# Three layout turns taken off TensorE: VectorE 32x32 block transposes with a DRAM shuffle, and a new slot order

## The reference, cut to what matters

```python
k = x @ Wk.T; v = x @ Wv.T                  # 16 heads of 32
k = k * cos + rotate_half(k) * sin
W = eye(32)                                  # per sequence and head
for each chunk of 16 tokens (256 in a row):
    z = kc @ W                               # this is the layer's output
    W = W - kc.T @ ((z - vc) * 2 / (16 * 32))
out = layernorm(z) * gamma + beta
x = layernorm(x + out @ Wo.T)
g = silu((x @ gate_w.T) * gate_s); u = (x @ up_w.T) * up_s
x = layernorm(x + ((g * u) @ down_w.T) * down_s)
```

## Time and profile before

| | us |
|---|---|
| median of 3 runs | 2064.01 (2063.62 to 2065.9) |
| the profiled execution, its own time | 2065.75 |
| its span in the trace | 2063.9 |
| TensorE (PE) busy | 1941.2, 94% |
| VectorE (DVE) busy | 1244.6, 60% |
| ScalarE (ACT) busy | 927.6, 45% |
| GpSimd (POOL) busy | 594.0, 29% |
| DMA, mean | 94 GB/s |

### The profile page before, as it was taken

The page is one execution under the profiler, slowest core; times in us unless marked ns, Lnnn a source line. Parts: engine busy times, 40 slices in busy tenths (PEclk is TensorE's granted clock), DMA queues, the critical chain, the costliest instruction groups (busy, mean ns, idle before and its releaser), DMA issues.

```text
span 2063.9 us, 54584 instructions
## 1 busy us (share of the span) xinstructions
PE 1941.2 (94%) x22424; PEld 1533.9 (74%) x22424; DVE 1244.6 (60%) x2814; ACT 927.6 (45%) x2258; POOL 594.0 (29%) x651
## 2 busy tenths in 40 slices
PE   3459999999999999999999999999999999999987
PEld 2237777777877777777777777777777787777775
DVE  2565666666566666656666665666666566666642
ACT  2225444444444444444444444444444444444432
POOL 1012323323332322333223233323323332332332
PEclk8669999999999999999999999999999999999998
DMA  9522332222233222223322222322222232222210
GB/s 327 182 84 63 104 100 76 94 85 80 87 105 98 78 89 90 77 90 104 97 78 86 94 75 92 104 90 84 88 88 81 91 104 90 81 90 73 85 41 21
DMA packets 236619, 193.38 MB, mean 94 GB/s; under 512 B 35217, under 2 KB 199313, under 8 KB 236177
## 3 DMA queue, kind: packets, MB, share of 16 engines
q1 hardware_dynamic: 233648, 172.56, 26.5%
q10 hardware_dynamic: 2720, 17.30, 2.3%
HBM read 105.86 MB, written 92.54 MB: 96 GB/s over the span
## 4 chain that ended last, share of the span: by engine, by line
PE 82%; DVE 7%; ACT 4%; issue 2%; DMA 2%; SPq 1%; POOL 0%; DVEq 0%; POOLq 0%; ACTq 0%
PE gu_acc L615 29%; PE work L596 26%; PE down_acc L627 15%; PE z_acc L569 4%; PE state_acc L584 4%; DVE err L795 3%; PE work L603 2%; ACT state L400 2%; PE gu_acc L603 2%; ACT hid L424 1%; DMA k_scr<-k_tok 1%; DVE fm L824 1%; DVE hid L802 1%; ACT fm L448 1%; SPq L230 1%
## 5 line engine op out<-in xcount | busy, mean ns | idle before, releaser
L795 DVE TENSOR_TENSOR err<-z_acc,v_rows 32x256 f32<-32x256 f32 x1024 | 429.6, 420 | 155.4 <-PE z_acc L569 105.7
L346 POOL TENSOR_TENSOR hid_lo<-hid,hid_hi 128x256 fp32r<-128x256 f32 x352 | 280.4, 797 | 777.3 <-ACT hid_hi L434 775.7
L400 ACT ACTIVATE state<-state_acc 32x256 f32<-32x256 f32 x1028 | 385.7, 375 | 197.5 <-PE state_acc L584 178.6
L615 PE MATMUL gu_acc<-x_hi,gw 128*128 128x256 f32 x1408 | 383.6, 305 | 6.8 <-DVE hid L802 3.3
L802 DVE SCALAR_TENSOR_TENSOR hid<-gu_acc,up_scale,hid 128x256 f32<-128x256 f32 x352 | 169.9, 483 | 297.8 <-ACT hid L424 293.9
L615 PE MATMUL gu_acc<-x_lo,gw 128*128 128x256 f32 x1408 | 347.6, 280 | 0.0
L615 PE MATMUL gu_acc<-x_lo,uw 128*128 128x256 f32 x1408 | 346.9, 279 | 0.0
L615 PE MATMUL gu_acc<-x_hi,uw 128*128 128x256 f32 x1408 | 346.9, 279 | 0.0
L615 PEld LDWEIGHTS gu_acc<-x_hi,gw 128*128 128x128 f32 x1408 | 264.8, 188 | 50.2 <-DVE hid L802 32.6
L627 PE MATMUL down_acc<-dw,hid_hi 128*128 128x512 f32 x704 | 289.8, 412 | 1.4 <-POOL hid_lo L346 1.4
L627 PE MATMUL down_acc<-dw,hid_lo 128*128 128x512 f32 x704 | 278.8, 396 | 0.0
(11 more groups left out here) (67 smaller groups left out, 2224.0 us busy)
## 6 DMA issues: line engine op xcount, KB each, us to landing
x_fm<-xT SPq DMA_DIRECT2D x64, 256.0 KB, 3.3
k_scr<-k_tok SPq DMA_DIRECT2D x32, 512.0 KB, 3.0
k_rows<-k_scr SPq DMA_DIRECT2D x512, 32.0 KB, 2.0
v_rows<-v_scr SPq DMA_DIRECT2D x512, 32.0 KB, 1.9
z_scr<-v_rows SPq DMA_DIRECT2D x32, 512.0 KB, 2.9
z_tok<-z_scr SPq DMA_DIRECT2D x512, 32.0 KB, 1.8
x_tok<-x SPq DMA_DIRECT2D x32, 512.0 KB, 3.9
out<-x_tok SPq DMA_DIRECT2D x32, 512.0 KB, 2.9
```

The lines of the kernel that those rows point to most:

```text
L346: pool.tensor_tensor(hid_lo[m % RING][:], hid[m % 2][:], hid_hi[m % RING][:].bitcast(F32), ALU.subtract).then_inc(hid_lo_ready, 1)
L400: act.activation(state[q, :, e].rearrange("p (r g) e -> p r g e", r=2), state_acc[q, :, 0:P].rearrange("p r (g e) -> p r g e", e=HEAD), AC ...
L615: mm = pe.matmul(gu_acc[:, k * TOK:(k + 1) * TOK], lhsT=w[:, c, m * P:(m + 1) * P].bitcast(dt), rhs=part[:, c].bitcast(dt), start=(c == 0 ...
L795: dve.tensor_tensor(err[q, g:g + 2, :, :].rearrange("p a (r h) e -> p a r (h e)", r=2), z_acc[q, :, 0:P].rearrange("p r (a c) -> p a r c", ...
```

## The change

- The 24 TensorE transposes of a tick are gone. VectorE turns 32x32 blocks (`turn`, one instruction for each b, six in a tick) from SBUF into one buffer, `turned`. SP stores it to DRAM in four transfers, one for each group of 32 partitions (`store_turned`), and loads it back in one, with the blocks in their places: `kT` for K, `landed` for z and for x1. A 128x128 turn is 16 block turns and this exchange of blocks.
- GpSimd copies `kT` to `k_cols` (now one buffer, in halves) in place of VectorE. `high_zn`, `low_zn`, `high_x1`, `low_x1` read SBUF (`landed`) in place of PSUM.
- New slots. Most of the feed-forward of block t-2 moves a tick later: in the tick that does its second norm only pieces 0 and 1 (slots 14, 15) remain. The b = 0 projections of block t move to the end of the tick ahead. The last norm of a block, `normalize(2, ...)`, moves from slot 14 to slot 0 of the next tick.
- The loops run from tick -1 to NT + 3, where they ran from 0 to NT + 2.
- SP issues 15 more transfers in a tick, and its order is new.

```diff
-FFN_SLOT = 10
-EARLY_GU, LATE_GU = {10: 0, 11: 1, 12: 2, 13: 3, 14: 4, 15: 5}, {0: 6, 1: 7, 2: 8, 3: 9, 6: 10}
+FFN_SLOT = 14
+EARLY_GU, LATE_GU = {14: 0, 15: 1}, {0: 2, 2: 3, 3: 4, 5: 5, 7: 6, 8: 7, 9: 8, 10: 9, 11: 10}
+EARLY_DOWN, LATE_DOWN = {15: 0}, {0: 1, 2: 2, 3: 3, 5: 4, 8: 5, 9: 6, 10: 7, 11: 8, 12: 9, 13: 10}
...
-            for t in range(NT + 3):
+            for t in range(-1, NT + 4):
                 tick(t)
...
+            def store_turned(scr, stored):
+
+                for a in range(HQ):
+                    sp.dma_start(scr[:, :, a].rearrange("h d g t -> d h (g t)"),
+                                 turned[a * HEAD:(a + 1) * HEAD].rearrange("d h g t -> d h (g t)")).then_inc(stored, 16)
...
+            def load_znT(n):
+                sp.wait_ge(znT_stored, 64 * (n + 1))
+                if n >= 1:
+                    sp.wait_ge(x1_lo_ready, 2 * n)
+                sp.dma_start(landed[:].rearrange("p a g t -> p (a g t)"),
+                             zT_scr.rearrange("h d a g t -> (h d) (a g t)")).then_inc(znT_in, 16)
...
+            def copy_k_cols(n, half):
...
+                a = slice(half * HQ // 2, (half + 1) * HQ // 2)
+                for p in range(2):
...
+                    pool.tensor_copy(dst, src).then_inc(k_cols_ready, 1)
...
+            def turn(src, b, done):
+
+                dve.transpose(turned[:, :, b * NC:(b + 1) * NC, :],
+                              src[:, b, :].rearrange("p (c h d) -> p h c d", c=NC, h=HQ)).then_inc(done, 1)
...
-                dve.tensor_tensor(x1_lo[:, :, b, :], gu_acc[:].rearrange("p (c t) -> p c t", c=NC),
-                                  x1_hi[:, :, b, :].bitcast(F32), ALU.subtract).then_inc(x1_lo_ready, 1)
+                dve.tensor_tensor(token_blocks(x1_lo, b), by_token(landed, b),
+                                  token_blocks(x1_hi, b).bitcast(F32), ALU.subtract).then_inc(x1_lo_ready, 1)
...
+                    if within(yn) and s == 0:
+                        normalize(2, yn, y_tok, y_tok, y_ready)
+                    if within(o) and s == 2:
+                        turn_zn(o, 0)
+                        turn_zn(o, 1)
...
+                    if within(t) and s == 6:
+                        turn_k(t, 0)
+                        turn_k(t, 1)
+                    if within(o) and s == 9:
...
+                        normalize(1, o, x1_tok[o % 2], x_tok, x1_ready)
+                        turn_x1(o, 0)
+                        turn_x1(o, 1)
```

More of the change, by code:

```diff
@@ L86, in build @@
         v_rows = sb("v_rows", [P, NS, 2, P])
-        k_cols = [sb(f"k_cols{i}", [P, NG, NS, 2 * MB]) for i in range(2)]
+        kT = sb("kT", [P, HQ, NG, HEAD])
+        k_cols = sb("k_cols", [P, HQ, NG, 2, 2 * MB])
         err = sb("err", [P, NG // 2, HQ, HEAD])
@@ L94, in build @@
         x1_tok = [sb(f"x1_tok{i}", [P, BATCH, DM]) for i in range(2)]
+        turned = sb("turned", [P, HQ, NG, HEAD])
+        landed = sb("landed", [P, HQ, NG, HEAD])
         x1_hi = sb("x1_hi", [P, NC, BATCH, P], F32R)
@@ L321, in tick @@
                 if within(sc):
-                    load_x(sc)
+                    load_v_half1(sc)
+                if within(o):
+                    load_x(o)
+                if within(t):
+                    store_v(t, 0)
+                if within(o):
+                    store_znT(o)
+                if within(t):
+                    store_k(t)
+                if within(o):
+                    load_znT(o)
+                if within(t):
+                    store_v(t, 1)
+                if within(sc):
+                    store_z(sc, 0, NS // 2)
+                if within(t):
+                    store_kT(t)
+                if within(sc):
+                    load_z(sc, 0, NS // 2, 16)
+                if within(t):
+                    load_kT(t)
+                    load_k_half0(t)
+                if within(o):
+                    store_x1T(o)
+                if within(t):
+                    load_v_half0(t, 0)
+                if within(o):
+                    load_x1T(o)
+                if within(t):
+                    load_v_half0(t, 1)
+                if within(t + 2):
+                    load_x_fm(t + 2)
+                if within(sc):
+                    store_z(sc, NS // 2, NS - 1)
+                    load_z(sc, NS // 2, NS - 1, 32)
+                    store_z(sc, NS - 1, NS)
+                    load_z(sc, NS - 1, NS, 48)
             run(tick)
@@ L599, in project @@
                     mm.then_inc(done, 1)
-            def turn(acc, src, b, done):
-                for c in range(NC):
-                    mm = pe.transpose(acc[:, c * P:(c + 1) * P], src[:, b, c * P:(c + 1) * P], eye[:])
-                mm.then_inc(done, 1)
             def gate_up(n, m, dt):
@@ L720, in tick @@
                         down(f1, EARLY_DOWN[s], ffn_dt)
-                    if t == 0 and s == 14:
-                        find_bias()
+                    if within(t + 1) and s in (13, 14):
+                        project_v(t + 1, 0, *((0, 3), (3, NC))[s - 13])
             def rest(ffn_dt):
                 tick(2, ffn_dt, FFN_SLOT, SLOTS)
-                for t in range(3, NT + 3):
+                for t in range(3, NT + 4):
                     tick(t, ffn_dt)
+            tick(-1)
             tick(0)
@@ L741, in _, with stats_of, moments_of @@
         def _(dve):
-            def moments_of(norm, n, src):
-                for b in range(BATCH):
-                    dve.bn_stats(stats[:, norm, b, :], src[:, b, :]).then_inc(stats_done[norm], 1)
+            def stats_of(norm, b, src):
+                dve.bn_stats(stats[:, norm, b, :], src[:, b, :]).then_inc(stats_done[norm], 1)
+            def moments_of(norm, n):
                 dve.wait_ge(stats_done[norm], 2 * n + 2)
@@ new lines, in tick @@
+                    if within(t + 1) and s == 11:
+                        low_x(t + 1, 1)
+                    if within(t + 1) and s == 13:
+                        rotate(t + 1, 0)
+                    if within(yd) and s == 13:
+                        scale_y(yd)
+                    if within(o) and s == 13:
+                        low_x1(o, 0)
+                        low_x1(o, 1)
+                    if within(yd) and s == 15:
+                        dve.wait_ge(y_added, 2 * yd + 2)
+                        stats_of(2, 0, y_tok)
+                        stats_of(2, 1, y_tok)
+                        moments_of(2, yd)
@@ L876, in tick @@
+                    if within(f2) and s in LATE_GU:
                         scale_hid(f2, LATE_GU[s])
-                    if within(f2) and s == 7:
-                        scale_hid(f2, 10)
                     if within(f1) and s in EARLY_GU:
@@ L916, in tick @@
                             low_part(wo, x1_tok, c, 2 * NC)
[L917 to L920 removed]
+                    for piece in WEIGHED.get((t, s), ()):
+                        weigh(piece)
+                    if t == 2 and s == 13:
                         dve.wait_ge(low_half_max, len(PIECES))
```

439 lines of the change are left out of this document (214 added, 225 removed).

## The result

Median of 4 runs 2123.12 us (2121.03 to 2128.82) against 2064.06 (2063.62 to 2065.9) for the kernel before: ratio 1.0289, 95% interval 1.0273 to 1.0306. The prediction said faster: 2018, with a range of 1981 to 2068. The direction, the size and the range were wrong.

A forecast was written before the change was run, and what follows sets the result against it. TensorE was taken to bound 28 or so of 35 ticks. Ticks 3 to 30 (-51.2), tick 31 (-3.6), start (-4) and tail (+12.8) took 2065.75 to 2019.75; the median, 1.7 lower, gave 2018, range 1981 to 2068.

The forecast's parts named there:

- The floor, 57.3: Middle tick: TensorE's 59.87 us of work less 2.6 for six transpose groups leaves 57.3 us.
- The block turn, 0.69: VectorE: each turn instruction takes 0.69 us, taken from another 128x512 float32 instruction; bounds 0.5 to 1.4.
- The rival of a slow turn: Slots 2, 7 and 9: turns of 1.4 us each lose 3.05 us a tick, giving 2106 us; chance 0.09.
- Slots 3 and 9, 0.45 and 0.37: Middle tick: TensorE waits for VectorE's `scale_hid`, 0.45 us ahead of slot 3's `gate_up` and 0.37 ahead of slot 9's.
- The z norm beside GpSimd's copy: Slots 0 to 3: VectorE's z norm meets GpSimd's K copies and ends at 7.4 us in place of 7.1.
- Slots 14 and 15, 0.1 + 0.2 + 0.1: Middle tick: TensorE stalls 0.1 us for slot 14's silu and `scale_hid`, 0.2 for slot 15's `copy_v`, 0.1 for `low_x1`.
- The rival that named it, 2047: x1's split meets GpSimd's residual add: `low_x1` pair ends 1.0 us later in 29 ticks, 2047 us; chance 0.19.
- z's detour, slack 1.4: Middle tick: turned z goes through DRAM and lands at 18.5 us, `high_zn` comes at 19.9; slack 1.4, cost nothing.
- The start, -4: First errors to tick 3's, 117.9 us before: 4 us shorter, ends -12 and +8.
- Tick 31 and the tail, -3.6 and +12.8: Tick 31 becomes 3.6 us shorter; the tail, where nothing hides the detours of z and x1, 12.8 longer.

The follow-up runs named there:

- e4_slots_only: Changed kernel with the second z turn, x1 turns and second norm's moments behind a `scale_hid`, half its statistics behind the scan's errors; 2104.32 us.
- e5_both: e1_late_residual plus the VectorE reordering of e4_slots_only; 2026.44 us.
- e2_memset: Changed kernel with GpSimd's residual add left out and a memset of a constant into the same tile in its place; 2045.29 us, one run.
- e1_late_residual: Changed kernel with GpSimd's residual add waiting until `low_x1` of the block behind it is done; 2044.89 us.
- e6_start: e5_both with the first weighing, VectorE's part of the reduction, the all-reduce and the FFN's loads some slots sooner; 2011.00 us.
- e10_z_before_k: e6_start with the load of the turned z issued on SP ahead of K's 512 KB store; 2009.35 us.
- e7_z_sooner: e5_both with VectorE's last norm behind the moments of z, and SP's loads of V and x moved around z's stores; 2064.44 us.
- e12_z_first: e10_z_before_k with VectorE's last norm behind z's moments, V's row loads ahead of out's store, x's load behind z's load; 2006.08 us.

## Why the prediction was wrong, point by point

- **The floor, 57.3.** Right: 57.29 to 57.39 of TensorE's work wherever the clock stayed at 1.00, and in the changed kernel 58.83 less the 1.5 that the slow `gate_up` took.
- **The block turn, 0.69.** Right: 0.682 to 0.691 in all three uses. The rival of a slow turn falls.
- **Slots 3 and 9, 0.45 and 0.37.** Right in place and nearly in size: 0.51 and 0.56. By e4_slots_only and e5_both both are worth 18 to 19 us together. The z norm beside GpSimd's copy was put 0.3 later; its pair took 1.13 against 1.00 for x's, so 0.13.
- **Slots 14 and 15, 0.1 + 0.2 + 0.1: the step that failed.** "`low_x1` ends when slot 14's `gate_up` wants it: 0.1" stands on a split at its free 0.69. It took 1.5, the wait was 1.96 in place of 0.1, and in 19 of 28 ticks the clock took 1.5 more, for which the sum had no term. Slot 15's 0.2 wasn't seen. The tick is then 57.3 + 0.51 + 0.56 + 1.96 + 1.5 = 61.8, measured 61.86; the mean of 61.58 has the ticks in which the clock held. With its clock this step makes most of the 91 us that the 29 ticks lie above the forecast.
- **The rival that named it, 2047.** The mechanism was there with its place, and got 0.19, priced at 1.0 a tick; measured 3.5 where the clock fell and 3.0 in the mean (1.96 and 1.04). Two errors made this. First the hold: GpSimd's pair was itself slowed (2.96 in place of 2.6), and the split ended 0.55 behind it, not 0.3. Second, and larger, the price ended with the wait. In the earlier trace rows there is already a `gate_up` of 3.16 behind an idle TensorE, and the windows of the start and the last tick have clocks of 0.78 and 0.90: a wait of 2 us should have been priced with the slow work behind it. With 3.0 in place of 1.0 the rival would have come to 2047 + 29 x 2.0 = 2105; the start and the tail, 7 and 11 above the forecast, are the other 18.
- **Its chance.** The norm beside two adds (2.92 against 0.99) was evidence that such a meeting costs a factor. The walk itself put both pieces into the same 2.6 us. Taking the two together, this should have been the forecast. The norm has one operand in SBUF beside its scalars, the split two, so the row showed such a hold but not that of the split. The Trainium skill (SBUF — State Buffer, Who interferes with whom) says it in a rule: two SBUF inputs on VectorE contend with a GpSimd instruction that reads SBUF. The trace agrees, 1540 ns against 688, and the write-only instruction of e2_memset leaves it at 688.
- **z's detour, slack 1.4.** The steps of the stores were too short. In the tick shown the four took 2.7 to issue (1.8 predicted) and had landed 4.8 after the first issue (3.6); the load took 3.5 (3.9). About 0.7 of slack was left there. In five other ticks of the changed kernel z was late, by 0.25 to 1.77 us and 4.0 in all, with the clock at 1.00 behind each; so "cost nothing" held nearly, and by a margin half as wide as forecast. With the other waits gone it is what remains (12 to 23 us of idle in e1_late_residual, e5_both, e6_start and e10_z_before_k).
- **The start, -4.** +3.0. The all-reduce beside TensorE's wait (6.2 us, where some 5 was forecast) was there as said; e6_start, which moves it with the weighing and the loads, gives 11.9 back. What made the other terms come out 6 us worse has no run of its own.
- **Tick 31 and the tail, -3.6 and +12.8.** The tail was +23.8. e1_late_residual has 151.0 for it, 6.4 less than 157.4: the split meets the add in the last two ticks too. The clock behind the waits for z and x1 (`project_o` 4.61 in place of 2.99, `gate_up` 3.42 in place of 2.16 in e5_both) is 2.9 of the other 4.6; the rest has no run of its own.

The forecast less the failed step is e1_late_residual: 58.65 in most ticks against 58.5. By the profiled spans it lies 25 us above the forecast: 7 of start, 5 of tail, and 13 in ticks, most of it in those with a late z.

## What to carry to other kernels

When an operand of a VectorE instruction moves from PSUM to SBUF, look up what GpSimd does in the same microseconds; if it reads SBUF there, delay it until VectorE is through, which cost nothing here and gave 78 us. Price a wait of TensorE of 2 us as the wait and the slow work that can follow it (1.5 us here, behind 19 of 28 such waits), and shorten or fill it before shorter ones are mended; a fill much longer than the wait costs what it gives. In an in-order DMA queue see what a moved instruction's consumer stands in front of: two VectorE instructions of half a microsecond, moved, became 120 us through SP.

## What the runs showed of the hardware

- VectorE with two SBUF operands beside a GpSimd add: 1540 to 1557 ns against 688, and GpSimd 1493 against 1291. Beside a GpSimd memset (526 ns): 688. A VectorE norm beside GpSimd copies: 1.13 against 1.00 for the pair. Block turns of x1 beside such copies: 1.29 for the pair, 1.30 alone. `scale_hid`, with one tile in PSUM and one in SBUF, beside the residual add of the kernel before: 0.48, as alone.
- The granted clock behind a wait of TensorE went with the wait's length, but not by it alone. Counted in the changed kernel and the twelve experiments, between 190 and 1840 us, with the clock of the 3.7 us behind each wait: 51 waits of 0.9 to 1.6 us, all at 1.00; 95 of 1.6 to 2.5 us, 29 at 1.00 and 66 lower; 25 of over 2.5 us, all lower. Single places: behind 1.38 us the clock was 1.00; behind 1.93, 1.96 and 2.85 us the next group took 4.38 (in place of 2.99), 3.59 (2.08) and 4.61 (2.99). So a late transfer can cost only its own wait in one tick and 1.4 us more in the next, as in the 58.7 and 62.0 of e1_late_residual.
- The 512 KB load of z took 3.1 to 5.5 us from issue to landing in the middle ticks of the changed kernel (median 3.8), and 4.2 to 6.4 (median 5.4) in e7_z_sooner, where it was issued behind two transfers of 512 KB.
- What stays open: whether the old split, with `gu_acc` in PSUM, would have been free beside the add, since they never met (`scale_hid` was); what decides between the two levels of the clock behind the same 1.96 us; and why z still lands late in some ticks of e12_z_first and not in others (1.15 us of wait in one, none in its neighbours).
